# A decoder layer on one Trainium2 core: one of eight products per chunk moved from VectorE to GpSimd

## What is computed

```python
delta = softplus((x @ W_dtw.T) @ W_dt + b_dt)     # [64, 64, 128]
Bm, Cm = x @ W_B.T, x @ W_C.T                     # [64, 64, 16]
A = -exp(A_log)                                   # [128, 16]
def step(h, (d_t, b_t, c_t, x_t)):                # over the 64 tokens of a sequence
    h = exp(d_t[..., None] * A) * h + d_t[..., None] * b_t[:, None, :] * x_t[..., None]
    return h, sum(h * c_t[:, None, :], axis=-1)
y = layernorm(ys + Dp * x); attn = y @ W_out.T
x = layernorm(x + attn)
x = layernorm(x + gated_attention(x, ctx)); x = layernorm(x + experts(x))
```

## Time and profile before

| | |
|---|---|
| median of 3 runs | 683.97 us (679.31 to 686.4) |
| profiled execution, its own time | 689.37 us |
| its span in the profile | 687.8 us |
| PE busy | 542.6 us (79%) |
| DVE busy | 426.6 us (62%) |
| ACT busy | 322.0 us (47%) |
| POOL busy | 369.5 us (54%) |
| SSM stage, first product to last weighing | about 24 to 258 us |

### The profile page before, as it was taken

How to read it: one execution, slowest core, us unless ns; L and a number is a source line. 1 busy time by engine, 2 the same in 40 slices (tenths; PEclk the granted TensorE clock), 3 DMA queues, 4 the chain that set the end, 5 groups by cost and what they waited for, 6 DMA issues and landing times.

```text
span 687.8 us, 10788 instructions
## 1 busy us (share of the span) xinstructions
PE 542.6 (79%) x3387; PEld 385.0 (56%) x3387; DVE 426.6 (62%) x862; ACT 322.0 (47%) x727; POOL 369.5 (54%) x301
## 2 busy tenths in 40 slices
PE   2579999889998897976555699797979699999800
PEld 0234445344453455875544488686857588899700
DVE  1599999999999970478678555555625422222155
ACT  2475676867768644322112255454525133333327
POOL 1487979899798862115445433626354533323341
PEclk9999999999999997555555589898989899999955
DMA  4434434454553526545433926252535465798494
GB/s 151 139 110 155 163 140 156 142 170 153 171 170 123 198 66 108 104 62 85 87 72 107 247 70 210 90 181 96 190 111 170 143 192 185 233 305 285 165 254 116
DMA packets 83319, 104.51 MB, mean 152 GB/s; under 512 B 40784, under 2 KB 64592, under 8 KB 83136
## 3 DMA queue, kind: packets, MB, share of 16 engines
q1 hardware_dynamic: 74576, 90.99, 44.2%
q0 software_dynamic: 4320, 8.92, 3.8%
q10 hardware_dynamic: 4368, 3.93, 2.0%
HBM read 91.48 MB, written 12.34 MB: 151 GB/s over the span
## 4 chain that ended last, share of the span: by engine, by line
PE 33%; POOL 20%; issue 15%; DVE 12%; DMA 7%; ACT 3%; another core or an unknown queue 2%; SPq 1%; DVEq 0%; POOLq 0%; ACTq 0%
POOL hc L646 12%; PE pB L1071 10%; PE pq L1084 5%; PE py L826 4%; PE py L1071 3%; PE pa L987 3%; POOL y_dram L753 2%; DMA dx<-in_ctx_T 2%; ACT x_all L1465 1%; PE pq L1054 1%; DMA x_all<-y_dram 1%; POOL xg_dram L744 1%; PE pC L1026 1%; POOL bc_rest L602 1%
## 5 line engine op out<-in xcount | busy, mean ns | idle before, releaser
L646 POOL TENSOR_TENSOR hc<-h,Crep 128x1024 f32<-128x1024 f32 x64 | 149.6, 2355 | 16.1 <-DVE h L1515 14.8
L753 POOL DMA_INDIRECT y_dram<-dx,xin x71 | 68.7, 967 | 144.6 <-ACT dx L1386 135.8
L826 PE MATMUL py<-hc,ident 128*128 128x512 f32 x256 | 122.2, 605 | 8.0 <-POOL hc L646 8.0
L1071 PE MATMUL pB<-Crep,wslot 128*128 128x256 f32 (+1 forms) x556 | 118.0, 358 | 13.1 <-issue 10.2
L1071 PEld LDWEIGHTS pB<-Crep,wslot 128*128 128x128 f32 x556 | 89.7, 203 | 30.4 <-issue 15.1
L1506 DVE TENSOR_TENSOR u<-dx,pC 128x1024 f32<-128x1024 f32 x64 | 77.1, 1205 | 18.5 <-PE pC L815 18.4
L826 PEld LDWEIGHTS py<-hc,ident 128*128 128x128 f32 x256 | 47.4, 191 | 55.0 <-issue 38.8
L1515 DVE TENSOR_TENSOR_SCAN h<-pB,u 128x1024 f32<-128x1024 f32 x32 | 73.0, 2282 | 1.0 <-ACT pB L1204 0.6
L1515 DVE TENSOR_TENSOR_SCAN h<-pa,u 128x1024 f32<-128x1024 f32 x32 | 73.0, 2281 | 0.0
L1797 DVE TENSOR_TENSOR u<-u,pB 128x512 f32<-128x512 f32 x36 | 24.7, 687 | 77.7 <-PE pB L1071 41.4
L1797 DVE TENSOR_TENSOR Crep<-u,pB 128x512 f32<-128x512 f32 x35 | 24.0, 687 | 71.1 <-PE pB L1071 50.7
(11 more groups left out here) (225 smaller groups left out, 957.0 us busy)
## 6 DMA issues: line engine op xcount, KB each, us to landing
wslot<-in_expert_w SPq DMA_DIRECT2D x46, 768.0 KB
Crep<-c_dram SPq DMA_DIRECT2D x64, 512.0 KB, 3.8
h<-m_dram SPq DMA_DIRECT2D x16, 256.0 KB
xin<-xg_dram SPq DMA_DIRECT2D x25, 130.0 KB, 3.4
cT_st<-in_ctx_T SPq DMA_DIRECT2D x8, 256.0 KB, 4.2
dx<-in_ctx_T SPq DMA_DIRECT2D x8, 256.0 KB, 2.9
delta<-in_ctx_tok SPq DMA_DIRECT2D x32, 64.0 KB
hc<-y_dram SPq DMA_DIRECT2D x8, 256.0 KB, 8.4
```

Of the source, the lines that this page charges most:

```text
L646: nc.gpsimd.tensor_tensor(hc[:, K % 4], h[:, K % 3], Crep[:, K % 4].rearrange("p a t -> p (a t)"), ALU.mult).then_inc(hc_done, 1)
L753: nc.gpsimd.indirect_dma_start(out=y2_dram, out_offset=bass.IndirectOffsetOnAxis(ap=xin[:, i % NX, a, D:D + 1].bitcast(i32), axis=0), in_= ...
L826: last = nc.tensor.matmul(py[:], ident[:], hc[:, K % 4, i * CH:(i + 1) * CH], start=False, stop=(K % STEPS == STEPS - 1 and i == 1))
L1071: last = nc.tensor.matmul(bank[:, o * a * P:(o + 1) * a * P], wslot[:, i % NW, stage * F + f * P:stage * F + (f + 1) * P], xgT[i % 2][:, 0 ...
```

## The change

In each chunk the product of step k = 4 (`U4`) is made by GpSimd instead of VectorE. Its B rows are not spread by TensorE: SyncE loads them from DRAM by a broadcast into `Brep`, which is a part of `wslot`. For this, `c_dram` now holds B and C (32 rows in place of 16), and the C loads read from row 16 on. `spreads(K)` counts the products that VectorE makes below K, since the counters `u_done` and `B_spread` now skip one in eight.

```diff
+        Brep = wslot[:, 0, 0:2 * CH].rearrange("p (a t) -> p a t", a=2)
-        c_dram = nc.dram_tensor("c_dram", (NCH, N, CH), f32, kind="Internal").ap()
+        c_dram = nc.dram_tensor("c_dram", (NCH, N2, CH), f32, kind="Internal").ap()
+        U4 = 4
+        def spreads(K):
+            return K - (K + STEPS - 1 - U4) // STEPS
 # SyncE
-                sp.dma_start(c_dram[c], bc_raw[N:N2]).then_inc(C_stored, 16)
+                sp.dma_start(c_dram[c], bc_raw[:]).then_inc(C_stored, 16)
+            def load_B(c):
+                sp.wait_ge(C_stored, 16 * (c + 1))
+                if c:
+                    sp.wait_ge(u4_done, c)
+                sp.dma_start(Brep, c_dram[c:c + 1, 2 * U4:2 * U4 + 2].broadcast_to([P, 2, CH])).then_inc(B_in, 16)
             store_C(0)
+            load_B(0)
             for c in range(NCH):
                 for k in range(STEPS):
                     load_C(STEPS * c + k)
                     if k == 4 and c + 1 < NCH:
                         store_C(c + 1)
+                    if k == 5 and c + 1 < NCH:
+                        load_B(c + 1)
 # GpSimd
                 if c >= 2:
-                    pool.wait_ge(u_done, STEPS * (c - 1))
+                    pool.wait_ge(u_done, spreads(STEPS * (c - 1)))
+                    pool.wait_ge(u4_done, c - 1)
+            def product_4(c):
+                K = STEPS * c + U4
+                pool.wait_ge(B_in, 16 * (c + 1))
+                pool.wait_ge(dx_done, c + 1)
+                if K >= 3:
+                    pool.wait_ge(h_done, K - 2)
+                nc.gpsimd.tensor_tensor(u[:, K % 3].rearrange("p (a t) -> p a t", a=2),
+                                        dx[:, c % 2].unsqueeze(1).to_broadcast([P, 2, CH]), Brep, ALU.mult).then_inc(u4_done, 1)
                     weigh_state(STEPS * c + k)
+                    if k == U4 - 3:
+                        product_4(c)
 # TensorE
                 if K:
-                    pe.wait_ge(u_done, K)
+                    pe.wait_ge(u_done, spreads(K))
-                    if K + 2 < STEPS * NCH:
+                    if K + 2 < STEPS * NCH and (K + 2) % STEPS != U4:
                         spread_B(K + 2)
 # ScalarE
-                    act.wait_ge(B_spread, STEPS * (c - 1))
+                    act.wait_ge(B_spread, spreads(STEPS * (c - 1)))
 # VectorE
-                dve.wait_ge(B_spread, K + 1)
+                dve.wait_ge(B_spread, spreads(K) + 1)
-                dve.wait_ge(u_done, K + 1)
+                if K % STEPS == U4:
+                    dve.wait_ge(u4_done, K // STEPS + 1)
+                else:
+                    dve.wait_ge(u_done, spreads(K) + 1)
-                    if K + 1 < STEPS * NCH:
+                    if K + 1 < STEPS * NCH and (K + 1) % STEPS != U4:
                         product(K + 1)
                     scan(K)
```

More of the change, by code:

```diff
@@ L257, in decoder_layer @@
         B_spread = sem("B_spread")
+        B_in = sem("B_in")
+        u4_done = sem("u4_done")
         a_ready = sem("a_ready")
@@ L457, in load_C @@
                     sp.wait_ge(hc_done, K - 3)
-                sp.dma_start(Crep[:, K % 4], c_dram[c:c + 1, 2 * k:2 * k + 2].broadcast_to([P, 2, CH])).then_inc(C_in[K % 4], 16)
+                sp.dma_start(Crep[:, K % 4], c_dram[c:c + 1, N + 2 * k:N + 2 * k + 2].broadcast_to([P, 2, CH])).then_inc(C_in[K % 4], 16)
+            def load_B(c):
[3 more added lines that the diff above has]
+                sp.dma_start(Brep, c_dram[c:c + 1, 2 * U4:2 * U4 + 2].broadcast_to([P, 2, CH])).then_inc(B_in, 16)
             def load_context(c):
@@ L495, in load_heads @@
                 else:
-                    sp.wait_ge(u_done, STEPS * NCH)
+                    sp.wait_ge(u_done, spreads(STEPS * NCH))
                 sp.dma_start(cTc, ctx_T[:, tokens(c)]).then_inc(heads_loaded, 16)
```

## The result

| | before | after |
|---|---|---|
| median | 685.18 us (679.31 to 689.16, 4 runs) | 700.89 us (699.36 to 704.98, 4 runs) |
| ratio, 95% interval | | 1.0264 [1.0221, 1.0306] |
| the same two in a later comparison | 683.59 us (29 runs) | 697.45 us (6 runs), 1.0184 [1.0133, 1.0235] |
| profiled execution, span | 689.37, 687.8 us | 700.91, 699.1 us |

The kernel is slower, by 15.7 us in the first comparison and 13.9 in the later one; the forecast was +14.8, thus 698.8 us, and 700.89 were measured. The ratios are not the quotients of the medians beside them, which are 1.0229 and 1.0203. The two profiled executions lie only 11.5 us apart, since that of before was 4.2 above its median. Lines have moved: L620 is now the remainder, L657 GpSimd's product, L674 the weighing, L845 the spread, L856 the sum, L1536 VectorE's product and L1548 its scan.

The account below looks back on a forecast made before the run. The prediction took a loop from GpSimd's remainder through weighing k = 4, TensorE and B/C to the next remainder as the bound. Product +16.3 and last chunk -1.5 gave +14.8 on 683.97, thus 698.8 us, range 694 to 704.

Parts of the forecast that it names:

- The loop: State-space stage: GpSimd work from remainder to weighing k = 4 (15.0 us) plus the way back (13.55) sets the chunk's 28.57 us.
- The product, 7 x 2.33 = 16.3: GpSimd's product behind weighing k = 1 lengthens each of seven chunks by 2.33 us, +16.3 us.
- The relief of VectorE and TensorE at nothing in chunks 0 to 6: VectorE's 1.11 us and TensorE's 0.59 us freed per chunk lie off the loop there and gain nothing.
- The new wait of scan k = 4, covered: VectorE waits 2.2 us for GpSimd before this scan, costing nothing since 1 us of cover remains.
- The last chunk, -1.5: Without a remainder there, the product costs nothing and TensorE's earlier work saves 1.5 us, between 0 and 2.2.
- Loads at nothing: Eight more 512 KB broadcasts in SyncE's queue and the larger B and C store cost zero.
- Shared port without effect: GpSimd's SBUF reads cost VectorE nothing, as its operations read PSUM; blocking would add up to 2.33 us per chunk.
- What would show it: Profile signs: remainders about 31.1 us apart, idle before them near 20 us, product 2.35 us, last chunk 1 to 2 shorter.
- VectorE waiting longer for TensorE before product k = 1: Profile sign: before product k = 1 of the next chunk, VectorE's wait for TensorE grows; no size given.
- The sum: Whole kernel: 16.3 - 1.5 = +14.8 us, on the profiled 689.37 us and on the median of 683.97 us.

Follow-up runs that it names:

- e1_idle_slot: Changed kernel with GpSimd's product moved between weighing k = 0 and the remainder, where GpSimd idled; 686.71 us, 1.0012 of the kernel before.
- e2_extra_loop: Kernel before plus one unused GpSimd product per chunk behind weighing k = 1, inside the loop; 702.13 us, 1.0254 of the kernel before.
- e10_bc_first: Kernel before with the next chunk's B/C product on TensorE moved ahead of the sum at k = 1; 685.25 us, 1.0012 of the kernel before.
- e4_no_product: Changed kernel without GpSimd's product and the B loads, so nobody makes product k = 4; 683.57 us, 0.9958 of the kernel before.
- e6_one_load: Changed kernel with only the first of its eight B loads; 678.23 us, 1.0168 of the kernel before.
- e5_dve_sbuf: Changed kernel with product k = 4 back on VectorE, still reading the B loaded into SBUF; 672.33 us, 1.0100 of the kernel before.
- e9_reorder_after: Changed kernel with two of TensorE's B spreads moved earlier and VectorE reading the gates one product later; 683.58 us, 1.0249 of the kernel before.
- e3_extra_idle: Kernel before plus one unused GpSimd product per chunk between weighing k = 0 and the remainder; 692.12 us, 1.0099 of the kernel before.
- e7_reorder: Kernel before with two of TensorE's B spreads moved earlier and VectorE reading the gates one product later; 669.21 us, 1.0045 of the kernel before.
- e11: Changed kernel with the next chunk's B/C product on TensorE moved ahead of the sum at k = 1; 689.68 us, 1.0089 of the kernel before.
- e12: Changed kernel with GpSimd's product ahead of the remainder and TensorE's B/C product ahead of the sum at k = 1; 682.76 us, 0.9964 of the kernel before.
- e13: Changed kernel measured again, unaltered, on the third group's chip; 697.45 us, 1.0184 of the kernel before.

## Why the prediction was right, and where its terms were off

- **The loop** (remainder, weighings, TensorE, B/C, next remainder): right. It is shown by e1_idle_slot (same work outside of it: nothing) and e2_extra_loop (other work inside of it: everything). What the prediction did not see is that a second path of nearly the same length lies beside it: to lengthen the loop costs nearly one for one (2.20 us of 2.32), to shorten it in the kernel before gains nothing (e10_bc_first).
- **The product, 7 x 2.33 = 16.3**: it measured 2.32 us, and the loop grew by 2.20 on average. With chunk 6, whose product stands behind the last remainder, that is 6 x 2.20 + 2.3 = 15.5. Of the 0.8 not even half is slack that I had seen and not subtracted, the 0.31 us before weighing 36: it stood in chunk 4 only, which grew by 1.97 us (30.54 instead of 28.57). The five others grew by 2.20 to 2.29, which is each time a little less than 2.33.
- **The relief of VectorE and TensorE at nothing in chunks 0 to 6**: right (e4_no_product, -0.05 per chunk).
- **The new wait of scan k = 4, covered**: right in its effect, off in size. I forecast 2.2 us for it; it is 1.5, for scan k = 3 had itself waited for ScalarE's exponentials (0.57 us in chunk 4), and so VectorE came to it later. Scan 36 starts 166.86 - 160.83 = 6.03 us after the remainder; 1.1 later than the old 4.93 was forecast.
- **The last chunk, -1.5**: the term that was mis-sized. From the last remainder to the context load it is 49.44 us after and 50.43 before; with the 2.3 us of chunk 6's product taken out, it gained 3.3. About half of it is the relief; e4_no_product, which has the relief alone, gained 3.3 too. The other half is not the work of the change: in the profile of before TensorE ran below full clock there (0.79 in 238:246), and its block of two sums took 5.07 us; in that of after it took 3.60. e2_extra_loop, without any relief, also had the last chunk 1.6 us shorter (51.09, of which 2.3 are its extra work). I had read no clock for that stretch. The profiled execution of before has a mean clock of 0.858 over its whole span; the executions of this kernel in the groups that follow have 0.857 to 0.878, so it is near the lowest, and the dip need not be typical. The rows of before, a window and the sums in it, then the sums of after:

```profile
238.00:246.00 8.00, 6.90 (x15) 3.01 (x16) 6.77 (x5) 3.37 (x6) 5.49 (x3) 0.79 0.49 166
```

```profile
240.72 5.07 PE L826 MATMUL py<-hc,ident 128*128 128x512 f32 x8
```

```profile
254.72 3.60 PE L856 MATMUL py<-hc,ident 128*128 128x512 f32 x8
```

- **Loads at nothing**: right (e6_one_load). **Shared port without effect**: right for the change, whose VectorE operations read PSUM (a scan takes 2.29 us as before); e5_dve_sbuf shows what it costs where both operands lie in SBUF.
- **What would show it**: remainders 31.1 apart (30.98), idle time before them near 20 us (20.4), the product at 2.35 (yes), TensorE idle before the sum of k = 4 (0.90): as said. VectorE's wait for GpSimd was 1.5 us and not about 2, and the last chunk shrank by 3.3 and not by 1 to 2. "VectorE waiting longer for TensorE before product k = 1" was wrong: 18.5 us against 18.4, because the whole chunk, product k = 1 with it, moved together.
- **The sum** for the profiled pair was +14.8 and it is +11.5 (+11.3 in the spans): the first remainder +0.3, the loop +15.5, the last chunk -3.3, later stages -1.2. The medians differ by 15.7 and 13.9. That these are nearer to the forecast than the profiled pair is in part luck: the profiled execution of before lies 4.2 us above its median. Between the two intervals, 1.0221 to 1.0306 and 1.0133 to 1.0235, there is little in common, though the quotients of the medians are near each other (1.0229 and 1.0203), and the two profiles of the changed kernel agree to 0.4 us on the end of this stage; why the ratios differ I can't say.

## What to carry to other kernels

Idle time of an engine with an in-order queue is a place and not an amount: find the wait in which it lies, and ask for each added instruction whether it stands ahead of that wait or behind it, on a loop through the other engines. Then test with an operation that nobody uses: put behind the wait and ahead of it, it gives the price of either place in two runs, before the real work is moved. Where a loop closes through several engines, shortening the wait of one of them (VectorE's, in e9_reorder_after) gives nothing as long as the next queue on the way (TensorE's) stays as long. And a shorter way back shows as a shorter chunk only if no other path is as long; measure the chunk by an operation that the edit did not move.

## What the runs showed that I had not expected

The clock granted to TensorE falls for some us in some executions, and I can't say why. Between 234 and 244 us it was 0.83 in the kernel before, 0.94 in e3_extra_idle, 0.88 in e7_reorder and 0.84 in e10_bc_first. All of these make every spread on TensorE and have no added GpSimd work inside the loop. The changed kernel, its repetition and all others (e1, e2, e4, e5, e6, e9, e11, e12) were granted 1.00 there. But these are single profiles, and one kernel can differ from itself: in 20:60 the changed kernel was granted 1.00 in its first profile and 0.91 in its second, with the same period. What TensorE did before it fell does not sort the kernels either: in 224:234 it was busy for all of the 10.00 us in before, e4_no_product and e12_bc_first_idle, and of these three the clock fell in the next 10 us only in before. More than single profiles speak for e10_bc_first: over the whole execution its 12 runs were granted 0.855 to 0.866, those of the kernel before on the same chip 0.861 to 0.873, and those of e11, e12 and e13 0.861 to 0.872. So it is shown that the order of the work on TensorE goes with a lower clock in this kernel; by which mechanism, and how much of its time that costs, stays open.
